# Attention scores as pairs of half-height products in a one-core transformer layer

## What is computed

```python
q_prime, k_prime = relu(q), relu(k)
q_cos, q_sin = q_prime * cos_w, q_prime * sin_w        # by position; the same for k
context = causal sum over earlier positions of (q_cos.k_cos + q_sin.k_sin) * v
norm    = causal sum over earlier positions of (q_cos.k_cos + q_sin.k_sin)
output  = context / (norm + 1e-6)
h = x + output @ out_w + out_b
return h + (gelu(rmsnorm(h) @ mlp_w1 + mlp_b1) @ mlp_w2 + mlp_b2)
# beside it: bitlinear(relu(bitlinear(x, w_fc) + gate * low_rank(x)) ** 2, w_proj)
```

## Time and profile before

| | before |
|---|---|
| median of 3 runs | 623.13 us |
| the profiled execution | 624.36 us |
| its span (first to last instruction) | 622.6 us |
| granted clock of TensorE, mean | 0.992 of full speed |
| TensorE busy, matmuls | 582.3 us, 94% |
| TensorE busy, weight loads | 514.3 us, 83% |
| VectorE / ScalarE / GpSimd busy | 409.4 / 365.1 / 221.5 us |
| score products (line 1250) | 256 of 128 rows x 256 columns |

### The profile page before, as it was taken

The page is one execution under the profiler, slowest core; times in us unless marked ns, Lnnn a source line. Parts: engine busy times, 40 slices in busy tenths (PEclk is TensorE's granted clock), DMA queues, the critical chain, the costliest instruction groups (busy, mean ns, idle before and its releaser), DMA issues.

```text
span 622.6 us, 14387 instructions
## 1 busy us (share of the span) xinstructions
PE 582.3 (94%) x5070; PEld 514.3 (83%) x5070; DVE 409.4 (66%) x776; ACT 365.1 (59%) x654; POOL 221.5 (36%) x251
## 2 busy tenths in 40 slices
PE   2758999999999999999999999999999999999996
PEld 2647798888898888988989888898889888898875
DVE  7698874586846856487746868378565878457542
ACT  5556665557645575466655576456754576555642
POOL 7007512444142720427124531436215251336220
PEclk9969999999999999999999999999999999999999
DMA  7772006500173004610065002620055000730001
GB/s 202 214 173 87 19 1 145 128 2 20 39 138 95 6 11 112 122 36 17 0 152 118 0 17 70 121 78 17 0 126 112 31 17 23 145 69 2 2 1 34
DMA packets 27993, 42.02 MB, mean 67 GB/s; under 512 B 9008, under 2 KB 19904, under 8 KB 27968
## 3 DMA queue, kind: packets, MB, share of 16 engines
q1 hardware_dynamic: 26528, 39.59, 27.5%
q10 hardware_dynamic: 1440, 2.10, 1.3%
HBM read 12.31 MB, written 4.19 MB: 27 GB/s over the span
## 4 chain that ended last, share of the span: by engine, by line
PE 73%; DVE 9%; SPq 7%; ACT 4%; issue 3%; DMA 1%; ACTq 1%; DVEq 0%; POOL 0%; POOLq 0%
PE accum L1227 19%; PE dense L1212 8%; PE dense L1392 7%; PE shared L1250 5%; PE ctx_ps L1275 5%; SPq L355 5%; PE dense L1262 4%; PE dense L1123 4%; PE dense L1397 4%; PE shared L1365 3%; SPq L406 3%; PE shared L1137 2%; PE dense L1217 2%; PE ctx_ps L1286 2%; PE upd_ps L1300 2%
## 5 line engine op out<-in xcount | busy, mean ns | idle before, releaser
L974 DVE TENSOR_TENSOR wide_lo<-wide,wide_hi 128x512 fp32r<-128x512 f32 x128 | 94.7, 740 | 119.0 <-ACT wide_hi L692 100.2
L982 DVE TENSOR_TENSOR weighted<-shared,cst 128x512 f32<-128x512 f32 x128 | 83.0, 683 | 15.8 <-PE shared L1250 15.8
L689 ACT ACTIVATE wide<-dense,b 128x512 f32<-128x512 f32 x64 | 44.2, 690 | 82.9 <-PE dense L1397 82.6
L1227 PE MATMUL accum<-w_hi,wide_hi 128*128 128x256 f32 x256 | 72.7, 284 | 2.2 <-DVE wide_lo L974 2.2
L531 POOL TENSOR_TENSOR state<-state,added 128x544 f32<-128x544 f32 x32 | 43.8, 1370 | 81.1 <-DVE added L1004 80.8
L1227 PE MATMUL accum<-w_lo,wide_hi 128*128 128x256 f32 x256 | 71.8, 280 | 0.0
L1227 PE MATMUL accum<-w_hi,wide_lo 128*128 128x256 f32 x256 | 71.7, 280 | 0.0
L497 POOL TENSOR_TENSOR arena<-arena,tab 128x256 f32<-128x256 f32 x64 | 49.6, 803 | 49.7 <-DMA q_stack<-arena 49.7
L1227 PE MATMUL accum<-prT,wide_hi 128*128 128x256 f32 x256 | 65.9, 286 | 1.2 <-DVE wide_lo L974 1.2
L1227 PE MATMUL accum<-prT,wide_lo 128*128 128x256 f32 x256 | 64.5, 281 | 0.0
L679 ACT ACTIVATE wide<-dense,scales 128x512 f32<-128x512 f32 x64 | 44.0, 687 | 33.4 <-PE dense L1217 33.4
(11 more groups left out here) (174 smaller groups left out, 1481.9 us busy)
## 6 DMA issues: line engine op xcount, KB each, us to landing
k_stack<-weighted SPq DMA_DIRECT2D x96, 128.0 KB, 2.6
q_stack<-arena SPq DMA_DIRECT2D x184, 64.0 KB, 2.3
xin<-L_attn_x SPq DMA_DIRECT2D x16, 256.0 KB, 2.9
out<-late SPq DMA_DIRECT2D x16, 256.0 KB, 2.3
tab<-trig SPq DMA_DIRECT2D x8, 258.0 KB, 2.6
arena<-L_ffn_w_fc SPq DMA_DIRECT2D x1, 1024.0 KB, 8.8
late<-L_ffn_w_proj SPq DMA_DIRECT2D x1, 1024.0 KB, 7.4
late<-L_attn_mlp_w ACTq DMA_DIRECT2D x1, 1024.0 KB, 5.3
```

Of the source, the lines that this page charges most:

```text
L689: act.activation(wide[:, m % 2, :], dense[m % 2][:, :], ACT.Gelu_apprx_tanh, bias=b1[:, m:m + 1]).then_inc(dense_free, 1)
L974: dve.tensor_tensor(wide_lo[:, n % 2, :], wide[:, n % 2, :], wide_hi[:, n % 2, :].bitcast(F32), ALU.subtract).then_inc(lo_done, 1)
L982: dve.tensor_tensor(weighted[:, g, :].rearrange("p (a n) -> p a n", a=4), shared[g % 2][:, :].rearrange("p (a n) -> p a n", a=4), mask.rea ...
L1227: mm = pe.matmul(accum[k // 2][:, (k % 2) * E:(k % 2 + 1) * E], a[:, n % 2, tok], w[:, n % HB, :], start=(first and i == 0 and k % 2 == 0) ...
```

## The change

`q_stack` loses its dimension r: its 128 rows hold both heads, with no zero half. `stack_q` becomes one transfer of 32 rows instead of two of 16, so 12 transfers per step instead of 24 (4 on ScalarE in the setup instead of 8); what is zeroed at the start is half as much. A call `scores(j, d)`, d = 0 or 1, makes 8 products of 64 rows by 128 columns of weights by 128 streamed columns, in turn in the lower and the upper half of the array, the lower into bank `shared[0]` and the upper into `shared[1]`. It replaces two of the old calls; it waits until both banks are free, and both banks count as full with its last two products. The heads come out in another order, which `within` and `turn_context` take up.

```diff
-N_Q_LO = 8
-N_Q_HI = 8
+N_Q_LO = 4
+N_Q_HI = 4
...
-        q_stack = sb("q_stack", [P, 4, 2, KE, TOK], F32R)
+        q_stack = sb("q_stack", [P, 4, KE, TOK], F32R)
...
-            for r in range(2):
-                row = 32 * g + 16 * r
-                queue.dma_start(q_stack[64 * r + slot:64 * r + 64:4, g, r, :, :].bitcast(F32),
-                                q_parts[row:row + 16, part, :, :]).then_inc(done, 16)
+            queue.dma_start(q_stack[slot:P:4, g, :, :].bitcast(F32),
+                            q_parts[32 * g:32 * g + 32, part, :, :]).then_inc(done, 16)
...
-                def scores(j, g):
-
-
-                    bank = shared_bank(S_SCORE + 4 * j + g)
+                def scores(j, d):
+
+                    later(pe, shared_free, shared_use(t, S_SCORE + 4 * j + 2 * d + 1) - 1)
                     tok = slice(chunk_block(j) * P, (chunk_block(j) + 1) * P)
-                    if j == 0 and g == 0:
+                    if j == 0 and d == 0:
                         pe.wait_ge(k_stacked, (t + 1) * N_K_STACK * 16)
                         pe.wait_ge(q_lo_stacked, (t + 1) * N_Q_LO * 16)
-                    if j == 0 and g % 2 == 0:
-                        pe.wait_ge(q_hi_stacked[g // 2], (t + 1) * N_Q_HI * 16)
-                    for i in range(2):
-                        row, m = g // 2 * 2 + i, g % 2
-                        mm = pe.matmul(bank[:, i * 2 * P:(i + 1) * 2 * P].rearrange("p (r n) -> p r n", r=2),
-                                       k_stack[:, row, m, tok], q_stack[:, row, :, m, tok], start=True, stop=True)
-                    mm.then_inc(shared_full, 1)
+                    if j == 0:
+                        pe.wait_ge(q_hi_stacked[d], (t + 1) * N_Q_HI * 16)
+                    for m in range(KE):
+                        for i in range(2):
+                            cols = slice((2 * m + i) * P, (2 * m + i + 1) * P)
+                            for r in range(2):
+                                rows = slice(64 * r, 64 * r + 64)
+                                mm = pe.matmul(shared[r][:, cols], k_stack[rows, 2 * d + i, m, tok],
+                                               q_stack[rows, 2 * d + i, m, tok], start=True, stop=True,
+                                               skip_group_check=True)
+                                if m == KE - 1 and i == 1:
+                                    mm.then_inc(shared_full, 1)
...
                 scores(0, 0)
-                scores(0, 1)
                 ffn_up(1)

                 for j in range(NB):
-                    scores(j, 2)
                     ffn_down(j, (0, 1))
-                    scores(j, 3)
+                    scores(j, 1)
                     ffn_down(j, (2, 3))
...
                         scores(j + 1, 0)
-                        scores(j + 1, 1)
                     ffn_up(j + 2, (2, 3, 4))
```

More of the change, by code:

```diff
@@ L480, in x_plus_b2 @@
                                    ALU.add).then_inc(xb_done, 2)
-            pool.memset(q_stack[:, 0:2, :, :, :].rearrange("p g r m n -> p (g r m n)").bitcast(F32),
+            pool.memset(q_stack[:, 0:2, :, :].rearrange("p g m n -> p (g m n)").bitcast(F32),
                         0.0).then_inc(stack_zero, 1)
@@ L578, in _ @@
             act.activation(first_act[:, :], half[:, :], ACT.Copy)
-            act.activation(q_stack[:, 2:4, :, :, :].rearrange("p g r m (a n) -> p (g r m a) n", n=P),
-                           ones[:, :].rearrange("p (a n) -> p a n", a=1).broadcast_to([P, 2 * 2 * KE * TOK // P, P]),
+            act.activation(q_stack[:, 2:4, :, :].rearrange("p g m (a n) -> p (g m a) n", n=P),
+                           ones[:, :].rearrange("p (a n) -> p a n", a=1).broadcast_to([P, 2 * KE * TOK // P, P]),
                            ACT.Copy, scale=0.0).then_inc(stack_zero, 1)
@@ L1284, in turn_context @@
                     for g in range(4):
-                        h = g % 2 * (H // KE) + g // 2 * 4
-                        mm = pe.matmul(ctx_ps[:, h * 32:h * 32 + P], ctxT[:, g * P:(g + 1) * P], ident,
+                        four = ctx_ps[:, :].rearrange("p (m d i r e) -> p m d i r e", m=KE, d=2, i=2, r=2)
+                        mm = pe.matmul(four[:, :, g // 2, :, g % 2, :], ctxT[:, g * P:(g + 1) * P],
+                                       ident.rearrange("p (m i e) -> p m i e", m=KE, i=2),
                                        start=False, stop=(g == 3), is_transpose=True, skip_group_check=True)
```

2 lines of the change are left out of this document (1 added, 1 removed).

## The result

The changed kernel takes 637.59 us, the median of 4 runs (636.61 to 638.80), beside 623.52 for the kernel before in the same comparison: a ratio of 1.0232, with a 95% interval of 1.0216 to 1.0248. It is slower by 2.3%, and the predicted 637.6 was met. As will be seen, the price of the change of partition was right, while several smaller terms of the sum were off and their errors cancel. That the time was met to 0.1 us is luck.

A forecast was written before the change was run, and what follows sets the result against it. TensorE, busy 94% of the span, was taken as the bound. Six steps 10.7, last step 2.1, step 0 2.15, setup -0.45 gave +14.5 us: 637.6 against the median; forecast 634 to 641 (0.60), range 626 to 650 (0.80).

The forecast's parts named there:

- The change of partition: On TensorE, going to 128-column weights costs 0.09 us of emptying plus 0.11 of bare load, 0.20 in all.
- The pair: Two half-height products side by side take 0.11 us, set by their weight loads; four pairs 0.44 against 0.47.
- Rivals 1: Loads of the two array halves don't overlap, so a pair takes 0.22 us: 664 us, chance 0.10.
- 4 (0.06): Half loads are quicker too, pair 0.06 us: 628 with emptying (chance 0.05), 608 without (0.02).
- rival 3: No emptying, and loads pulled ahead between whole and half-height mode: faster, 621 us, chance 0.08.
- rival 2: A change of partition costs only the bare load, or only one way: 628 to 633 us, chance 0.09.
- Block 0 of each step: The calls of scores at j=0, with VectorE's delay of ffn_down(0), make TensorE 0.72 us later.
- (a): At j=0, filling both banks in one call delays VectorE's split and holds ffn_down(0) 0.07 us more; nothing more.
- Rival 5: Later completion of scores opens missed waits on VectorE in every iteration: 642 to 650 us, chance 0.06.
- The wait of `across(1,0)`: In steps 1 to 6 TensorE's 0.89 us wait for the context on VectorE absorbs 0.30 of the delay.
- The transfers at 0: SyncE's 12 issues instead of 24 end 7.5 us sooner, delaying only GpSimd's products for across: 0 us.
- (c): In step 0, paced by VectorE, weigh(0,2) waits 0.9 us, j=1 brings it to 1.25, later blocks to 2.15.

The follow-up runs named there:

- e5: Changed kernel with each of its 32 calls scores(j,1) cut in two, so 64 more changes of partition for the same products: 648.22 us, ratio 1.0406.
- e4: Changed kernel with the 8 half-height products of a call replaced by 4 of 128 rows by 128 by 128 columns (scores wrong): 627.17 us, ratio 1.0072.
- e6: Changed kernel with each half-height product streaming 64 instead of 128 columns, half of the scores left out: 636.78 us, ratio 1.0220.
- e1: Kernel before, its products and 24 transfers kept, but called in the changed kernel's order, one call filling and awaiting both banks: 629.13 us, ratio 1.0104.
- e8: Kernel before with only the load of the next step's x moved from SyncE to ScalarE: 621.69 us, ratio 0.9976.
- e2: Changed kernel with q_stack filled by 24 transfers of 16 rows again: 637.30 us, ratio 1.0223.
- e3: Changed kernel where GpSimd's first product for across also waits for VectorE's last split of the step before: 637.46 us, ratio 1.0229.
- e7: Kernel before with the load of x issued by ScalarE and GpSimd's addition of x and its bias in step 0 one wait later: 623.39 us, ratio 0.9999.

## Why the prediction was right, and where only the sum was

**The change of partition (right).** Predicted 0.09 + 0.11 = 0.20 one way, from column strips and one product of 16 rows. Measured: 0.08 to 0.09 before the first load on both sides of a call, 0.90 for a whole call against 0.91, 0.43 per block against 0.455 (0.325 + 0.13), and 0.34 per added change there and back in e5. e4 takes the changes away, together with half of the products, and the 0.43 is gone (-0.05 to -0.07); e5 adds changes alone, with the products as they were, and each costs what was forecast. Of the 14.1 us between the medians 10.4 lie between e4 and the changed kernel.

**The pair (right).** 0.11 with the two loads side by side, as the strip loads of `update` had suggested; e6 shows that the stream has no part in it. Rivals 1 (0.22) and 4 (0.06) fall by that, rival 3 by the gaps, rival 2 because the gap is paid both ways.

**Block 0 of each step (mis-sized).** The forecast had 0.65 for its two calls and 0.07 for (a), 0.72 in all. Measured 1.02 to 1.07 ahead of `across(0,0)` in steps 3 to 6. The step that failed is (a), "nothing more": the wait of `scores(0,0)` for the second bank and the waits queued behind it weren't in it (0.27 in the changed kernel), nor that of `scores(0,1)` for `weigh(0,1)` (about 0.1 in e1). The terms don't simply add: the placement alone costs 0.7 there (e4), and the two calls' changes of partition add 0.33 to that and not 0.65, partly because the 0.09 ahead of `scores(0,0)` falls into its wait. Rival 5 named such waits, in every iteration, and asked 5 to 12 us for them; it was half right, at about 2 us.

**The wait of `across(1,0)` (right in kind, too small).** Predicted to shrink from 0.89 to 0.6, so that 0.30 is absorbed. Its row in the changed kernel's step 3:

```profile
282.81 0.96 PE L1277 MATMUL ctx_ps<-state,arena 128*128 128x136 f32 x6 [0.44 <-DVE late L992]
```

0.45 was absorbed, and from `across` of block 0 to that of block 1 the steps 1 to 6 cost nothing at all (-0.03 to -0.01).

**The transfers at 0 (wrong).** The forecast asked who waits for the queue and named GpSimd's products for `across` alone. The load of x stands behind the queue as well (e8), and of the products the question was what they run beside once they don't wait. It costs 0.24 to 0.27 per step through VectorE (e2, e3), 0.21 as a mean behind the last `across` in steps 3 to 6. So these are 1.79 + 0.32 (block 0) - 0.17 (more absorbed) - 0.06 (the two blocks behind, 0.43 instead of 0.455 each) + 0.21 (collision) = 2.09, measured 2.08.

**Steps 1 and 2 (not foreseen).** They cost 1.2, since the wait for x absorbs 0.9 in each. The six steps come to 1.17 + 1.23 + 4 x 2.08 = 10.7, which was the predicted figure, by two errors that cancel.

**Step 0 (wrong: 2.15 predicted, 0.27 and 0.08 measured).** The delays (c) were worked out on the timeline of VectorE in step 0. The first of them came as forecast: `weigh(0,2)` is 0.9 later in the step. But behind the row at 49.67 stand the cast and the split of a part of w2, and their lengths were taken as their own:

```profile
50.87 1.01 DVE L860 CAST w_hi<-late 128x512 fp32r<-128x512 f32 x1
51.91 1.65 DVE L862 TENSOR_TENSOR w_lo<-late,w_hi 128x512 fp32r<-128x512 f32 x1
```

1.56 us of this were GpSimd's: in e7, where its addition runs elsewhere, they take 0.41 and 0.69. In the changed kernel GpSimd's addition is over before them, and they take 0.42 and 0.69:

```profile
52.15 0.42 DVE L858 CAST w_hi<-late 128x512 fp32r<-128x512 f32 x1
52.60 0.69 DVE L860 TENSOR_TENSOR w_lo<-late,w_hi 128x512 fp32r<-128x512 f32 x1
```

With 24 transfers (e2) step 0 costs 1.03, still less than half of what was predicted. VectorE reaches the cast later there too, so that only the end of GpSimd's addition falls on it, and nothing on the split:

```profile
51.64 1.27 DVE L860 CAST w_hi<-late 128x512 fp32r<-128x512 f32 x1
```

The later blocks of step 0 were also put too high: the two behind `across(1,0)` cost 0.15 and 0.33 in the changed kernel, 0.16 and 0.33 in e2, instead of 0.455 each. In the changed kernel GpSimd is earlier because the query stack is: its products start at 43.80 instead of 46.31, and its addition at 48.21 instead of 50.29 (two rows, of the changed kernel and of the kernel before):

```profile
43.80 4.45 POOL L495 TENSOR_TENSOR arena<-arena,tab 128x256 f32<-128x256 f32 x4 [30.77 <-DMA q_stack<-arena]
```

```profile
46.31 2.20 POOL L497 TENSOR_TENSOR arena<-arena,tab 128x256 f32<-128x256 f32 x2 [32.89 <-DMA q_stack<-arena]
```

**The setup (wrong: -0.45 predicted, +0.34 and +0.14 measured).** ScalarE's reads of fcT came at 33.15 (32 to 33 was said), and the transposes of w_proj started at 40.91 instead of 41.47, 0.56 sooner. But then they ran longer. The windows (from:to, length, TensorE's busy time with its number of instructions, granted clock as a share of 2.4 GHz, the transfers' share and rate), of the kernel before:

```profile
42.00:43.00 1.00, 1.00 (x7) 0.53 0.83 328
43.00:44.00 1.00, 1.00 (x10) 1.00 1.03 377
```

of the changed kernel:

```profile
42.00:43.00 1.00, 1.00 (x6) 0.50 0.22 74
43.00:44.00 1.00, 1.00 (x7) 0.50 0.02 8
44.00:45.00 1.00, 0.55 (x3) 0.50 0.00 0
```

and of e2, the changed kernel with 24 transfers:

```profile
42.00:43.00 1.00, 1.00 (x8) 0.57 0.89 360
43.00:44.00 1.00, 0.92 (x9) 1.00 0.95 344
```

In both with 24 transfers TensorE's clock is back at 2.4 GHz at about 43, when the second eight transposes run (1.04 us for them). With 12 it is still at 1.2 GHz, and they take 1.92:

```profile
42.64 1.92 PE L1188 MATMUL accum<-cst,late 128*128 128x128 f32 x8
```

That is 0.88 lost against 0.56 gained. What the engine did before: in the kernel before its work on fcT and gT had just been held up, so that it was busy for 3.3 of the 4 us from 38 to 42; in the changed kernel that work had come earlier, it was busy for 2.0 of these 4 us, and it had been idle for 2.0 us when the transposes started. The same difference stands in all twelve traces: a slow second half in the six with 12 transfers (1.58 us in e6 to 1.92), a fast one in the six with 24 (1.04 to 1.12). That the earlier work is the cause is inferred from these; no run moved it by itself. The setup also varies for reasons that have nothing to do with the change: in e1 the first eight transposes ran at 2.4 GHz too (1.06 us), and in e3 a load came late.

**The time.** The profiled span grew by 13.2, 1.3 less than the sum; between the medians lie 14.1, since the one profiled execution of the kernel before was 0.84 slow. Step 0 and the setup took 1.1 less than forecast together, steps 3 to 6 took 1.2 more, steps 1 and 2 took 1.2 less and step 7 took 0.25 less. The forecast of 637.6 is closer to the median than its terms deserve.

## What to carry to other kernels

Before a product is cut into parts of the array, count the changes of partition and the weight loads: here a change there and back costs 0.34 us between whole products, and a pair of half-height products costs its load of 0.11 us at 64 streamed columns as at 128. Against whole products of 0.117 us the 256 pairs could win no more than 1.8 us even with no change at all (an estimate from these two figures), against 10.4 that the changes cost. Freeing a queue or an engine off the critical path isn't free: ask what the engine behind it will run beside, since the duration of a VectorE operation in a trace may belong to GpSimd. A wait that is put ahead of others holds these up as well. And a sum of small terms can meet the time by errors that cancel; subtract the traces stage by stage before believing it.

## What the runs showed of the hardware

The loads of a pair in the two halves of the array start 3 to 4 ns apart in the calls between whole products and then run side by side (0.18 to 0.19 each, eight in 0.52). Between whole and half-height products about 0.09 us pass in which nothing starts, both ways, as between whole products and column strips; from column strips to half-height products it is the same (the call behind `within` costs 0.59 in the chain, as the others do). VectorE's operations with two inputs in SBUF grow from 0.69 to 1.23 and 1.65 us beside GpSimd, and those on 128 x 4 elements from 0.15 to 0.76; a cast with one input of 128 x 512 grows from 0.42 to 1.01 in the kernel before and to 1.27 in e2. TensorE's sequencer took 0.3 us to pass three waits that had long been fulfilled, behind one that it had to wait for (e1). Where some work of TensorE at 1.2 GHz started 0.56 us sooner, the clock came back later, at 45.2 instead of 42.9 us, and more was lost than gained.
